# A decoder layer on one core: value products on four column groups, and another order for the last two base groups

## The reference

```python
def self_attention(x):
    q, k, v = split(x @ Wqkv.T + b)                  # q: 16 heads of 16; k, v: one head of 16
    scores = where(causal, q @ k.T / 4, min)         # per sequence and head, 128 x 128
    return (softmax(scores) @ v) @ out_w.T + out_b

def cross_attention(x, ctx):                         # keys and values are both ctx, 8 heads of 8
    return softmax(q @ k.T / sqrt(8)) @ v            # four query heads to each key head

def ffn(x):
    base = (silu(x @ gate) * (x @ up)) @ base_down
    w, idx = top_2(softmax(x @ gate_w)); w = w / w.sum()
    return base + sum_over_e(w_e * expert_e(x))

x = layernorm(x + self_attention(x))
x = layernorm(x + cross_attention(x, ctx))
x = layernorm(x + ffn(x))
```

## Time and profile before

| what | value |
|---|---|
| median of 3 runs | 708.4 us (706.02 to 711.39) |
| profiled execution | 704.1 us, of which its span is 701.9 us |
| mean granted TensorE clock | 0.957 |
| busy, share of the span | PE 89%, DVE 65%, ACT 48%, POOL 20% |
| attention | up to about 390 us |
| base groups and sorted tiles | about 390 to 660 us |
| last downward tiles, shares, layer norm, stores | about 660 to 702 us |

### The profile page before, as it was taken

How to read it: one execution, slowest core, us unless ns; L and a number is a source line. 1 busy time by engine, 2 the same in 40 slices (tenths; PEclk the granted TensorE clock), 3 DMA queues, 4 the chain that set the end, 5 groups by cost and what they waited for, 6 DMA issues and landing times. The chain is left out here.

```text
span 701.9 us, 11383 instructions
## 1 busy us (share of the span) xinstructions
PE 627.2 (89%) x3351; PEld 425.6 (61%) x3379; DVE 458.5 (65%) x1020; ACT 333.9 (48%) x705; POOL 142.7 (20%) x159
## 2 busy tenths in 40 slices
PE   2767999999999999999887798999999999999981
PEld 2444455555455555555433576888888788887770
DVE  3479889888988888988764583344343344344296
ACT  2355777777777777776744311132322232223114
POOL 2033110111110111110100002143433343341000
PEclk9889999999999999999968799999999999999996
DMA  8104443324443234443320681016436653110703
GB/s 263 36 1 158 157 158 128 105 102 163 166 166 131 82 119 165 165 159 121 135 98 14 230 331 31 16 53 214 170 120 223 224 165 108 47 52 19 239 1 120
DMA packets 54440, 90.47 MB, mean 129 GB/s; under 512 B 6284, under 2 KB 25231, under 8 KB 54384
## 3 DMA queue, kind: packets, MB, share of 16 engines
q1 hardware_dynamic: 50640, 80.43, 33.2%
q0 software_dynamic: 3744, 9.31, 4.2%
HBM read 56.18 MB, written 34.47 MB: 129 GB/s over the span
## 5 line engine op out<-in xcount | busy, mean ns | idle before, releaser
L1169 ACT ACTIVATE silu<-inner 128x512 f32<-128x512 f32 x55 | 32.9, 598 | 159.7 <-PE inner L1550 110.6
L486 ACT ACTIVATE prob<-scores 128x1024 f32<-128x1024 f32 x96 | 98.4, 1027 | 13.0 <-PE scores L859 8.6
L1329 DVE TENSOR_TENSOR hT<-hiddenT,hT 128x512 fp32r<-128x512 f32 x39 | 27.0, 692 | 87.9 <-ACT hT L1175 87.9
L632 DVE TENSOR_REDUCE max_c<-scores 128x8 f32<-128x1024 f32 x64 | 78.0, 1218 | 8.8 <-PE scores L922 7.2
L1545 PE MATMUL inner<-weights,sT_hi 128*128 x156 | 68.7, 440 | 0.3
L946 PE MATMUL sums<-prob,v_c 128*32 128x512 f32 x256 | 66.9, 648 | 0.0
L1135 POOL DMA_INDIRECT chosen_y<-lane_hot,to_row x39 | 40.0, 1026 | 132.2 <-DVE lane_hot L1344 132.2
L1546 PE MATMUL inner<-weights,sT_hi 128*128 x156 | 61.5, 394 | 0.0
L398 POOL TENSOR_TENSOR xT_lo<-xT_in,xT_hi 128x256 fp32r<-128x256 f32 x16 | 11.9, 745 | 236.1 <-ACT xT_hi L457 236.1
L1129 POOL DMA_INDIRECT rows<-x,from_row x39 | 38.2, 979 | 87.8 <-DVE from_row L1311 76.2
L932 PE MATMUL scores<-q_c,k_c 128*128 128x512 f32 x128 | 46.5, 445 | 5.9 <-ACT prob L486 2.8
(11 more groups left out here) (218 smaller groups left out, 1430.0 us busy)
## 6 DMA issues: line engine op xcount, KB each, us to landing
split_w<-halves SPq DMA_DIRECT2D x32, 768.0 KB, 5.3
weights<-split_w SPq DMA_DIRECT2D x8, 3072.0 KB, 12.8
raw_w<-in_expert_w SPq DMA_DIRECT2D x16, 768.0 KB, 4.6
weights<-chosen_y SPq DMA_DIRECT2D x8, 512.0 KB, 7.5
xT_in<-in_xT SPq DMA_DIRECT2D x16, 128.0 KB, 4.6
x_in<-in_x SPq DMA_DIRECT2D x16, 128.0 KB, 3.6
x<-stream SPq DMA_DIRECT2D x16, 128.0 KB, 4.6
ctxT_in<-in_ctxT SPq DMA_DIRECT2D x16, 96.0 KB, 4.0
```

The lines of the kernel that those rows point to most:

```text
L486: act.activation(prob[:, m, :], scores[:, n, :], ACT.Exp, scale=scale).then_inc(sem[exped], 1)
L632: dve.tensor_reduce(out_[:, 8 * unit:8 * unit + 8], scores[:, n, :].rearrange("p (h k) -> p h k", k=S), AX.X, ALU.max).then_inc(sem[read], 1)
```

## The change

Attention. All four column groups of PE get a value product of their own. `s_sum` is one stage in place of two: four products of 32 rows, two halves by two values of b. `c_sum` is two stages of four products in place of four of two; both write the same bank, the second accumulates onto the first. For that the value tile `v_c` is laid out so that the second half's values stand 16 columns further within their group of 32, and the columns of the other half are zero. So there is one bank of sums for each kind of attention and sequence: `s_read`, `c_read`, `s_out` and `c_out` on PE, `s_den` and `c_den` are one in place of two, and DVE's `s_out` and `c_out` stay two instructions. The tables change with it, as do the counts at which slots are released.

Experts. `base_hT` has eight slots in place of five. PE runs all upward chunks of groups 2 and 3, then all eight downward tiles. DVE adds shares 0 to 5 between the multiplications of group 3 and the rest between the takes.

```diff
-HT_RING = 5
+HT_RING = 8
@@ PE_ORDER @@
-    ("c_sum", 1, -1), ("s_main", 1, 2), ("c_shift", 0, 0), ("c_sum", 2, -1), ("s_max", 0, 3), ("c_sum", 3, -1),
-    ("c_main", 0, 0), ("c_out", 0, -1), ("s_sum", 0, 2), ("c_main", 1, 0), ("c_out", 1, -1), ("s_max", 1, 3),
+    ("c_sum", 0, -1), ("s_main", 1, 2), ("c_shift", 0, 0), ("s_max", 0, 3), ("c_sum", 1, -1),
+    ("c_main", 0, 0), ("c_main", 1, 0), ("c_out", 0, -1), ("s_max", 1, 3),
...
-PROB_USE = {"s_exp": ("s_summed", 2), "c_exp": ("c_summed", 4)}
+PROB_USE = {"s_exp": ("s_summed", 1), "c_exp": ("c_summed", 2)}
...
@@ PE @@
+            def s_sum(seq, unit):
+
+                p, n = seq.odd, sum_ring.slot("s_sum", 0, seq)
+                wait(pe, sem["s_exp"], seq, 2)
...
                 for h in range(2):
-                    mm = pe.matmul(sums[64 * h:64 * h + 64, n, :], v_s[p][:], prob[:, m, 512 * h:512 * h + 512], start=True, stop=True)
+                    for b in range(2):
+                        at = 64 * h + 32 * b
+                        mm = pe.matmul(sums[at:at + 32, n, :], v_s[p][:], prob[:, prob_ring.slot("s_exp", b, seq), 512 * h:512 * h + 512],
+                                       start=True, stop=True)
...
+            def c_sum(seq, a):
...
+                for j in range(4):
+                    m, v = prob_ring.slot("c_exp", 2 * a + j // 2, seq), j % 2
+                    mm = pe.matmul(sums[32 * j:32 * j + 32, n, :], v_c[p][:, P * a + 32 * j:P * a + 32 * j + 32],
+                                   prob[:, m, 512 * v:512 * v + 512], start=(a == 0), stop=(a == 1))
@@ experts, DVE @@
+            next_up = u + CHUNKS - 1
+            multiply(next_up)
+            add_shares(0)
+            multiply(next_up + 1)
+            for t in (1, 2):
+                add_shares(t)
+            multiply(next_up + 2)
+            for t in (3, 4):
+                add_shares(t)
+            multiply(next_up + 3)
+            add_shares(5)
+            for m in range(2 * TILES):
                 take(first + m)
+                if m == 2 * TILES - 2:
+                    variance(0)
+                    newton(0)
+                if m < 2 * TILES - 1:
+                    add_shares(6 + m)
@@ experts, PE @@
-            base_chunk(GROUPS_FIRST + 1, 0)
+            for c in range(CHUNKS):
+                base_chunk(GROUPS_FIRST + 1, c)
             base_outer(GROUPS_FIRST)
-            for c in range(1, CHUNKS):
-                base_chunk(GROUPS_FIRST + 1, c)
             base_outer(GROUPS_FIRST + 1)
```

More of the change, by code:

```diff
@@ L55 @@
     ("s_proj", 0, 1), ("c_max", 2, 0), ("s_main", 0, 2), ("s_turn", 0, 3), ("c_max", 3, 0), ("s_res", 0, 1),
-    ("c_sum", 1, -1), ("s_main", 1, 2), ("c_shift", 0, 0), ("c_sum", 2, -1), ("s_max", 0, 3), ("c_sum", 3, -1),
-    ("c_main", 0, 0), ("c_out", 0, -1), ("s_sum", 0, 2), ("c_main", 1, 0), ("c_out", 1, -1), ("s_max", 1, 3),
-    ("c_turn", 0, 1), ("c_main", 2, 0), ("s_out", 0, 2), ("c_max", 0, 1), ("s_qkv", 0, 4), ("s_sum", 1, 2),
-    ("s_shift", 0, 3), ("c_main", 3, 0), ("s_out", 1, 2), ("c_max", 1, 1), ("c_sum", 0, 0),
+    ("c_sum", 0, -1), ("s_main", 1, 2), ("c_shift", 0, 0), ("s_max", 0, 3), ("c_sum", 1, -1),
+    ("c_main", 0, 0), ("c_main", 1, 0), ("c_out", 0, -1), ("s_max", 1, 3),
+    ("c_turn", 0, 1), ("c_main", 2, 0), ("c_max", 0, 1), ("s_qkv", 0, 4), ("s_sum", 0, 2),
+    ("s_shift", 0, 3), ("c_main", 3, 0), ("s_out", 0, 2), ("c_max", 1, 1),
     ("x2_logit", 0, -3), ("x2_turn", 0, -2),
@@ L63 @@
     ("s_proj", 0, 1), ("c_keys", 0, 1), ("s_turn", 0, 3), ("s_exp", 0, 2), ("c_log", 0, -2),
-    ("s_split", 0, 4), ("c_read", 0, -1), ("c_rsqrt", 0, -2), ("s_exp", 1, 2), ("s_log", 0, 1),
-    ("s_rsqrt", 0, 1), ("w_high", 0, 2), ("c_read", 1, -1), ("c_rows", 0, 1), ("c_exp", 0, 0), ("s_read", 0, 2),
-    ("c_exp", 1, 0), ("c_turn", 0, 1), ("c_exp", 2, 0), ("c_values", 0, 1), ("w_high", 1, 2), ("s_read", 1, 2),
+    ("s_split", 0, 4), ("c_rsqrt", 0, -2), ("s_exp", 1, 2), ("s_log", 0, 1),
+    ("s_rsqrt", 0, 1), ("w_high", 0, 2), ("c_read", 0, -1), ("c_rows", 0, 1), ("c_exp", 0, 0),
+    ("c_exp", 1, 0), ("c_turn", 0, 1), ("c_exp", 2, 0), ("c_values", 0, 1), ("w_high", 1, 2), ("s_read", 0, 2),
     ("c_exp", 3, 0), ("s_rows", 0, 4), ("x2_logit", 0, -3), ("x2_read", 0, -2),
@@ L69 @@
 DVE_ORDER = [
-    ("s_den", 1, 1), ("s_out", 1, 1), ("c_max", 1, 0), ("s_rows", 0, 3), ("s_proj", 0, 1),
+    ("s_den", 0, 1), ("s_out", 0, 1), ("c_max", 1, 0), ("s_rows", 0, 3), ("s_proj", 0, 1),
     ("c_max", 2, 0), ("c_aggr", 0, -2), ("c_keys", 0, 1), ("s_turn", 0, 3), ("c_max", 3, 0),
@@ L101 @@
     "s_shift": [("s_shift_read", 1, 1)],
[L102 removed]
+    "s_out": [("s_ctx", 1, 1)],
     "s_proj": [("s_ctx_read", 1, 1)],
```

153 lines of the change are left out of this document (67 added, 86 removed).

## The result

| what | before | after |
|---|---|---|
| median of 4 runs each | 707.2 us (705.6 to 711.4) | 742.8 us (739.5 to 758.6) |
| ratio, 95% interval | | 1.048 (1.040 to 1.056) |
| profiled execution, its span | 704.1, 701.9 us | 740.7, 738.8 us |
| mean granted TensorE clock | 0.957 | 0.915 |
| busy, share of the span | PE 89%, DVE 65%, ACT 48% | PE 81%, DVE 63%, ACT 43% |

The change makes the kernel 4.8% slower: 742.8 us, where 712 was forecast and the range ended at 729. By the interval of the ratio the loss is 28 to 39 us, and the two spans differ by 36.9. The attention alone loses more than that. One run of the changed kernel (758.6, at a clock of 0.890) stands apart and is left out of the ratio; without it the median is 740.7.

The account below looks back on a forecast made before the run. PE was taken to set the pace, DVE close behind. Twelve steps 0.85 us longer, less 1, gave attention +9; with -5.2 at the end, +4: 708 on the profiled execution, 712 on the shown median; range 699 to 729.

Parts of the forecast that it names:

- the last groups: End of the kernel, last two base groups: new order lets the last output end near 693.4 instead of 698.59, -5.2 us.
- the end of the attention: After the twelve full steps: both kernels wait on chains with one or two sums in them; 1 us taken off.
- Rival D: Value products on PE: four column groups run as two pairs, s_sum and c_sum(0) each 1.0 longer, +24, 736 us; chance 0.11.
- The walk to s_den: From DVE's second max_s to s_den: s_den starts at 7.00 us instead of 5.77, and DVE stands 1.5 us.
- The walk to c_sum(0): Later in the step, from s_proj to the context sum after s_res: unchanged order, 4.24 us, so c_sum(0) starts at 12.5.
- From q_c to the next second max_s 6.1: Last part of a step: 7.14 us falls by 1.1, plus 0.05 for a late rsqrt, making the step 22.05.
- Before them nothing: Attention steps ahead of the twelve with all stages: no loss, since c_sum is missing and so its hand-off is too.
- (b): One s_sum now after s_qkv: c_exp(2) waits for its slot, c_main(3) for c_exp(2); s_den 1.2 us late.
- (a): c_sum(0) now directly ahead of s_main(1): s_exp(0) waits for it, s_main(1) for s_exp(0); PE stands 1.1 us.
- B: Same as the main forecast, plus PE's clock falls in sparse stretches: +10 (every second step) to +19, 718 to 731; chance 0.25.
- A: Attention as worked out, with both hand-off stalls: steps of 21.8 to 22.3 us, 708 to 716 us; chance 0.50.
- C: Stalls do not bind and PE's saved time arrives: steps toward DVE's 19.2, 678 us, halfway 690 to 702; chance 0.14.

Follow-up runs that it names:

- the two runs with pairs: Kernel before, pair products kept: c_sum(0) moved directly ahead of s_main(1), 726.3 us; then s_sum(0) moved behind s_qkv as well, 750.8 us.

## Why the prediction was wrong

The place, the two hand-offs and the sign of the attention's part were right, and so was the sign of the last groups. The size of the attention's part was wrong: +38.3 us in place of +9. What failed are four terms of the sum: the clock, put at nothing (9.0 us); the steps ahead of the first c_ln, put at nothing (6.8 more than the forecast's two steps); the stretch from q_c to the next max_s, 6.1 us where it took 6.73, with a small delay ahead of it (9.2 in ten steps); and the end of the attention (3.4).

1. **Four side by side, 0.98 us: right.** From 193.34 the next product starts at 194.34, 1.00 us later. Rival D is out, and the 1.3 times that the forecast worked out from the Trainium skill (TensorE: Matmul & The Clock Gate, Part 3, "Measured speedup vs the span model", a row for row tiles) does not show here: four products free PE after 1.00 us and a pair after 0.98. A single product stands in no run.
2. **The walk to s_den: right.** Forecast 7.00 with a wait of 1.5; it stands at 197.66 - 190.55 = 7.11, with a wait of 1.56.
3. **The walk to c_sum(0): right.** Forecast 12.5, measured 203.21 - 190.55 = 12.66.
4. **c_sum, s_exp, s_main in a row: right.** From c_sum(0) to q_c 3.45 were forecast and 206.79 - 203.21 = 3.58 measured; both sums hand over after 1.19 to 1.20 us, not 1.08. With what was already late, q_c comes at 16.24, not 15.95.
5. **"From q_c to the next second max_s 6.1": wrong by 0.6.** It took 213.52 - 206.79 = 6.73: 0.50 is the lengthened t_c, which the two changed positions of DVE and POOL brought together, and 0.1 the wider reciprocal of 32 numbers. So the undisturbed step is 22.97 and not 22.05. In ten steps that is +9.2.
6. **"Before them nothing": wrong, +6.8.** The first c_ln is 8.5 us late, and 1.7 of that was forecast (two steps of 0.85). Hand-off (b) and the late s_den need only the self-attention, and they bind as soon as s_sum is there; two clock falls, at 67 and 101 us, are in it too. With (b) undone the first c_ln is back at 106.9 (107.1 before); with (a) undone it is at 111.0, 4.6 us earlier than in the changed kernel.
7. **The clock as a rival (B, 0.25) and not part of the forecast: this was the choice that failed.** The ten full steps took 238.7 us, against 229.7 for ten of 22.97: 9.0 us, for six falls. B had named the mechanism, the number (in every second step, six) and, at +10, the price, and the place too: its sparsest stretch, 3.9 to 7.9 us of the step, is that of 217 to 221. What B lacked was the second sparse stretch, at c_main(1). And B was added to a sum that was itself too short, so even its 731 was not enough.
8. **The end of the attention, "-1": +2.4**, with the clock low in much of it.
9. **The last groups, -5.2: measured -3.5.** The term "0.8 for the second downward tile" was 2.19, since the clock fell at PE's pause there. Where it did not fall, in the run with both hand-offs undone, the wait was 0.71 and the end 5.2 us shorter, as forecast: this term, too, is the clock's.

The differences of points 5 to 8 add up: 9.2 + 6.8 + 9.0 + 3.4 = 28.4, and 0.7 because the first of the ten intervals was 20.5 and not 21.2 before. That is the 29.1 between 9.2 (the forecast before rounding) and 38.3.

**The rivals.** A was the mechanism of the undisturbed steps, and undoing its two hand-offs removed 3.7 us a step. B came on top of it. C, that the saved work arrives, failed for this order of the tables and only for it: with the two sums in their old places the step is 19.2, and the kernel gains 3.5%. D is out.

Three things stay open: why ACT starts 0.25 us later behind c_sum's pair than behind a fourfold group, how the first steps' +6.8 divides between hand-offs and clock, and why the clock falls at one sparse stretch and not at the next like it.

## What to carry to other kernels

When two stages become one, ask at which of the two places the new one stands. A ring slot is freed by the last of its readers, and a merged reader put at the later place makes every writer of that slot late. Write down, for each moved stage, who waits for its slot and whether the next instruction on its own engine waits for that writer. Here, moving two entries of PE's table back (and one of ACT's) took the ratio from 1.048 to 0.965.

A price for hand-offs worked out at full clock can be too low when PE also has less to do. PE's full work with shorter pauses (the two runs with pairs, 2.2 and 3.4 us of standing a step) and less work with short pauses (the run with both undone, 2.1 us) left the clock of the full steps alone; less work and 5.8 us of standing cost 9 us more in ten steps. So put a fall into the sum, with its chance, wherever a change leaves PE such a sparse stretch.
